# Set-up in finer steps over four engines, norms by ScalarE, last rows through TensorE, and a new order in every queue

## The reference

```python
x = x + attn(layernorm(x)); x = x + ffn(layernorm(x))
# attn, per sequence of 512 rows
q = tanh(xn @ W_charge.T + b)[..., 0];  phi_c = mags * q ** arange(5)
shell = xn @ W_shell.T + b_shell;  shell = shell / max(norm(shell), 1e-12)
proj = shell @ omega.T + rff_bias
phi_s = concat([cos(proj), sin(proj)]) * rff_scale
phi = (phi_c outer phi_s).reshape(.., 320) @ W_combine.T
logits = phi @ phi.T * decay / (softplus(log_temp) + 0.1), causal
out = softmax(logits) @ (xn @ W_v.T + b_v) @ W_out.T + b_out
# ffn: route each row to 64 slots (hidden gelu layer, top 8, softmax = alpha),
# gather rows into slots, one GRU step per slot, spread slot values by alpha
```

## Time and profile before

| | |
|---|---|
| median of 3 runs | 716.89 us (716.38 to 717.22) |
| the profiled execution, its own time | 718.19 us |
| its span, first to last instruction | 716.4 us |
| busy share of the span: PE, DVE, ACT, POOL | 96%, 85%, 70%, 57% |
| mean granted clock of PE | 0.994 |
| stages in the span | set-up and prologue to 190.9, twelve turns of the loop to about 682, end to 716.4 |

### The profile page before, as it was taken

One profiled execution on the slowest core, in us unless ns is written; L12 is line 12 of the kernel. 1 busy time (PEld: TensorE's weight loads), 2 busy tenths in 40 slices (PEclk: granted clock), 3 DMA queues, 4 the chain that ended last, 5 costly groups with the idle time before them and its releaser, 6 DMA issues.

```text
span 716.4 us, 15768 instructions
## 1 busy us (share of the span) xinstructions
PE 686.0 (96%) x4652; PEld 545.1 (76%) x4652; DVE 605.6 (85%) x1996; ACT 498.2 (70%) x1239; POOL 408.5 (57%) x861
## 2 busy tenths in 40 slices
PE   8988999999999999999999999999999999998895
PEld 4766787877796977888797878779687777876774
DVE  5868978788989898998989898898989899787965
ACT  3758896958486786858677695858679685856441
POOL 4646577454565667475665757476565747635300
PEclk8999999999999999999999999999999999999999
DMA  8241111202332140423224051323205032121004
GB/s 251 81 148 40 50 29 32 60 1 88 92 117 60 57 123 2 130 47 119 59 77 102 1 156 23 118 61 114 63 31 146 4 118 60 61 59 60 1 28 150
DMA packets 49114, 54.11 MB, mean 76 GB/s; under 512 B 6212, under 2 KB 40582, under 8 KB 49030
## 3 DMA queue, kind: packets, MB, share of 16 engines
q1 hardware_dynamic: 48258, 52.58, 25.9%
q10 hardware_dynamic: 772, 0.53, 0.3%
HBM read 20.58 MB, written 16.78 MB: 52 GB/s over the span
## 4 chain that ended last, share of the span: by engine, by line
PE 62%; ACT 16%; issue 8%; POOL 6%; DVE 3%; DMA 3%; SPq 1%; ACTq 1%; DVEq 0%; POOLq 0%
PE ps L340 16%; PE ps L314 12%; PE ps L432 6%; PE ps L509 5%; PE ps L406 4%; PE ps L573 4%; PE ps L494 4%; PE ps L385 4%; POOL Z L251 2%; ACT L724 2%; ACT Eh L755 2%; DMA xmT<-Z 2%; PE ps L460 2%; ACT L776 2%; PE ps L387 2%
## 5 line engine op out<-in xcount | busy, mean ns | idle before, releaser
L678 ACT ACTIVATE xn<-X,rs 128x255 f32<-128x255 f32 x128 | 66.2, 593 | 77.7 <-POOL rs L1299 77.7
L251 POOL TENSOR_TENSOR Z<-Z,QB 128x512 f32<-128x512 f32 x60 | 77.1, 1286 | 73.8 <-ACT Z L734 71.3
L432 PE MATMUL ps<-Vh,Eh 128*128 128x256 f32 x320 | 96.0, 300 | 2.6 <-DVE El L934 2.0
L340 PE MATMUL ps<-W1h,xh 128*128 128x354 f32 x256 | 88.3, 345 | 1.5 <-DVE Vl L890 1.4
L432 PE MATMUL ps<-Vh,El 128*128 128x256 f32 x320 | 89.4, 279 | 0.0
L432 PE MATMUL ps<-Vl,Eh 128*128 128x256 f32 x320 | 89.4, 279 | 0.0
L340 PE MATMUL ps<-W1h,xl 128*128 128x354 f32 x256 | 83.1, 325 | 0.0
L340 PE MATMUL ps<-W1l,xh 128*128 128x354 f32 x256 | 83.1, 325 | 0.0
L890 DVE TENSOR_TENSOR Vl<-ps,Vh 128x256 fp32r<-128x256 f32 x128 | 53.3, 419 | 35.0 <-ACT Vh L700 33.9
L745 ACT ACTIVATE E<-ps,nmax 128x128 f32<-128x128 f32 (+3 forms) x128 | 67.7, 531 | 15.7 <-DVE nmax L926 15.3
L934 DVE TENSOR_TENSOR El<-ps,Eh 128x128 fp32r<-128x128 f32 (+3 forms) x128 | 60.8, 484 | 7.4 <-ACT Eh L755 7.3
(11 more groups left out here) (213 smaller groups left out, 1990.5 us busy)
## 6 DMA issues: line engine op xcount, KB each, us to landing
X<-in_x SPq DMA_DIRECT2D x32, 512.0 KB, 4.5
xmT<-Z SPq DMA_DIRECT2D x120, 128.0 KB, 2.3
out_x<-X SPq DMA_DIRECT2D x30, 512.0 KB, 3.5
out_x<-X SPq DMA_DIRECT2D x4, 256.0 KB, 3.2
X<-in_gru_whhT SPq DMA_DIRECT2D x1, 768.0 KB
wih<-in_gru_wihT SPq DMA_DIRECT2D x1, 768.0 KB
X<-in_W_v ACTq DMA_DIRECT2D x1, 256.0 KB, 4.4
X<-in_W_outT ACTq DMA_DIRECT2D x1, 256.0 KB, 5.6
```

Source lines behind the costliest of these rows:

```text
L251: e.tensor_tensor(Z[:, i + 1, :], Z[:, i, :], QB[:, :], ALU.mult).then_inc(s["zm"], 1)
L340: ins = e.matmul(p[:, 0:FEATS], x[:, d, c, t * 128:t * 128 + 128], w[:, c, :], start=j == 0, stop=j == 5)
L432: ins = e.matmul(p[:, 0:D], w[:, r % 2, j * 128:j * 128 + 128], v[:, (2 * k + d) % 4, j, :], start=z == 0, stop=z == len(parts) - 1)
L678: ins = e.activation(xn[:, d, t, 0:D - 1], X[:, b % NX, t, 0:D - 1], ACT.Identity, bias=rs[:, d, 2, t:t + 1], scale=rs[:, d, 1, t:t + 1])
```

## The change

It touches five things; the sizes of all tiles stay.

1. Set-up. ACT's queue issues W_v, W_out, b_v, b_out, omega; the biases of shell and charge go to SP's queue, ahead of the second x. The signals are split: wv (W_v, b_v), wa (W_out, b_out, omega), wsh (shell). PE can start the value products when wv and wa are there. The copy to W1 is gone: high parts are cast from PSUM, one half by DVE, one by ACT (`weights_high`); low parts are taken from PSUM. POOL's nine constants go first. DVE's set-up is cut into `bias_setup`, `temper_setup`, `attention_setup`, `slot_setup`, three `slot_values_setup` and others, placed between steps of pairs 0 and 1. ACT empties the six state products (`states_setup`). PE gets `keep_warm` (256-column matmuls on zeros, one and four of them).
2. Norms. `square` and `norm_sum` are gone. `v_high` copies 34 columns and squares the 64 shell columns with a sum (`accum_out`).
3. `sine` takes the Sin of the remainder first, then Abs, then the second Sin.
4. End. `warm` 3, 4, 21 and 2 become one `warm(12)`. `residual` puts the last two row tiles of X in PSUM by an identity matmul, `out_mm` adds to them, and DVE and ACT copy one each (`last_copy`) in place of two `finish`.
5. Every queue has a new order in prologue, loop and end.

```diff
@@ v_high (ACT)
-                    e.wait_ge(s["sq"], b - 1)
+                    e.wait_ge(s["n2"], 8 * k)
+                    e.wait_ge(s["q1"], k)
-                e.activation(F[:, d, t, :], at["vs", b, t][:, D:FEATS], ACT.Copy)
+                e.activation(F[:, d, t, 64:98], at["vs", b, t][:, D + 64:FEATS], ACT.Copy)
+                e.activation(F[:, d, t, 0:64], at["vs", b, t][:, D:D + 64], ACT.Square,
+                             accum_out=n2[:, d, 0, t:t + 1]).then_inc(s["n2"], 1)
@@ the end (PE)
+                    ins = e.matmul(p[:, :], ident[:, :], X[:, (2 * k + d) % NX, 2:4, :].rearrange("p t d -> p (t d)"),
+                                   start=True, stop=False, skip_group_check=True)
+                ins.then_inc(s["res"], 1)
@@ start of PE's queue, after
+            first_warm(); weights_setup(); keep_warm(1); xn_t(0, 0, 0); xn_t(0, 0, 1); keep_warm(4)
+            proj(0, 0, 0); xn_t(0, 1, 0); xn_t(0, 1, 1); proj(0, 0, 1); proj(0, 0, 2); proj(0, 0, 3)
+            proj(0, 1, 0); proj(0, 1, 1); proj(0, 1, 2); xn_t(1, 0, 0); xn_t(1, 0, 1); proj(0, 1, 3)
+            slot_setup(); gates_setup(); states_setup(); xn_t(1, 1, 0); proj(1, 0, 0); q_t(0); proj(1, 0, 1)
+            xn_t(1, 1, 1); proj(1, 0, 2); proj(1, 0, 3); z_t(0); proj(1, 1, 0); phi(0); proj(1, 1, 1)
+            logits(0, 0); proj(1, 1, 2); e_t(0, 0); e_t(0, 1); proj(1, 1, 3); logits(0, 1); e_t(0, 2)
@@ start of DVE's queue, after
+            clear_setup(); values_setup(); ln_stats(0, 0, 0); ln_stats(0, 0, 1); scale_a_setup()
+            shell_setup(); ln_stats(0, 1, 0); ln_stats(0, 1, 1); ln_stats(1, 0, 0); scale_b_setup()
+            weights_high(); ln_stats(1, 0, 1); weights_low(0); weights_low(1); xn_low(0, 0, 0)
+            xn_low(0, 0, 1); v_low(0, 0, 0); xn_low(0, 1, 0); xn_low(0, 1, 1); v_low(0, 0, 1); v_low(0, 0, 2)
+            bias_setup(); v_low(0, 0, 3); ln_stats(1, 1, 0); temper_setup(); ln_stats(1, 1, 1); v_low(0, 1, 0)
+            v_low(0, 1, 1); slot_setup(); v_low(0, 1, 2); xn_low(1, 0, 0); slot_values_setup(0)
@@ start of POOL's queue, after
+            scales_setup(); ln_scale(0, 0); ln_scale(0, 1); attention_setup(); ln_scale(1, 0); temper_setup()
+            slot_setup(); ln_scale(1, 1); rnorm(0); phase(0); ln_scale(2, 0); rnorm(1); phase(1)
@@ loop, PE
-                xn_t(p, 0, 0); xn_t(p, 0, 1); gx_rz(m); e_t(n, 0); proj(p, 0, 0); proj(p, 0, 1); proj(p, 0, 2)
-                proj(p, 0, 3); xn_t(p, 1, 0); xn_t(p, 1, 1); gx_n(m); values(n, 0); xm_t(f, 0, 0)
+                xn_t(p, 0, 0); xn_t(p, 0, 1); gx_rz(m); e_t(n, 0); e_t(n, 1); proj(p, 0, 0); proj(p, 0, 1)
+                xn_t(p, 1, 0); proj(p, 0, 2); xn_t(p, 1, 1); proj(p, 0, 3); gx_n(m); values(n, 0)
@@ loop, ACT, the part behind the first tiles
-                v_high(p, 1, 2); expo(n, 4); v_high(p, 1, 3); xm_copy(f, 1, 0); expo(n, 5); charge(p)
-                xm_copy(f, 1, 1); gelu(f, 0); probs_t(n, 3); probs_t(n, 4); q_copy(p); gelu(f, 1); sine(p)
+                probs_t(n, 2); v_high(p, 1, 1); expo(n, 5); v_high(p, 1, 2); v_high(p, 1, 3); charge(p)
+                xm_copy(f, 1, 0); xm_copy(f, 1, 1); gelu(f, 0); probs_t(n, 3); probs_t(n, 4); q_copy(p)
+                gelu(f, 1); sine(p); rt_out(f); probs_t(n, 5); z_copy(p); expo(n, 6); expo(n, 7)
@@ loop, DVE, the first part
-                finish(g, 0, 0); row_max(n, 1); row_max(n, 2); xn_low(p, 0, 0); xn_low(p, 0, 1); row_max(n, 3)
+                row_max(n, 1); row_max(n, 2); row_max(n, 3); finish(g, 0, 0); xn_low(p, 0, 0); xn_low(p, 0, 1)
@@ end, PE
-            gx_rz(14); hidden(15, 1); al_t(14); route(15); gx_n(14); rt_t(15); out_mm(13, 1); warm(21)
+            xm_t(15, 0, 0); xm_t(15, 0, 1); gx_rz(14); xm_t(15, 1, 0); xm_t(15, 1, 1); hidden(15, 0)
+            hidden(15, 1); al_t(14); route(15); gx_n(14); rt_t(15); out_mm(13, 1); warm(12); residual()
```

More of the change, by code:

```diff
@@ L582, in first_warm, with keep_warm @@
                     e.matmul(banks[2][:, :], E[:, 0, 0:128], E[:, 0, :], start=True, stop=True)
+            def keep_warm(n):
+                for _ in range(n):
+                    e.matmul(banks[2][:, 0:256], E[:, 0, 0:128], E[:, 0, 0:256], start=True, stop=True)
             def warm(n):
@@ L594, in weights_setup @@
                     cs = slice(c * 128, c * 128 + 128)
[L595 to L597 removed]
+                    p = at["setup_mm", c]
                     columns_of(p, 256, [(wsc[:, cs], ident[0:65, 0:65])])
@@ L639, in _ @@
-            proj(4, 1, 1); proj(4, 1, 2); values(3, 0); proj(4, 1, 3); logits(3, 1); out_mm(0, 0); gather(1)
-            e_t(3, 2); hidden(2, 0); q_t(4); values(3, 1); values(3, 2); xm_t(2, 1, 0); e_t(3, 3)
-            xm_t(2, 1, 1); logits(3, 2); values(3, 3); hidden(2, 1); out_mm(0, 1); gi_t(1); e_t(3, 4)
-            e_t(3, 5); route(2); z_t(4); rt_t(2); gx_rz(1); values(3, 4); gx_n(1); e_t(3, 6); values(3, 5)
-            e_t(3, 7); al_t(1); values(3, 6); slot_v(1); values(3, 7); phi(4); gather(2); logits(4, 0)
@@ new lines, in _ @@
+            values(1, 7); phi(2); xn_t(4, 0, 0); proj(3, 0, 3); logits(2, 0); xm_t(1, 0, 0); proj(3, 1, 0)
+            e_t(2, 0); proj(3, 1, 1); proj(3, 1, 2); xm_t(1, 0, 1); proj(3, 1, 3); e_t(2, 1); e_t(2, 2)
+            values(2, 0); logits(2, 1); gather(0); values(2, 1); e_t(2, 3); q_t(3); hidden(1, 0)
+            xm_t(1, 1, 0); xm_t(1, 1, 1); values(2, 2); values(2, 3); gi_t(0); e_t(2, 4); hidden(1, 1)
+            xn_t(4, 0, 1); e_t(2, 5); gx_rz(0); values(2, 4); route(1); logits(2, 2); gx_n(0); z_t(3)
@@ new lines, in _ @@
+            e_t(2, 6); values(2, 5); al_t(0); xn_t(4, 1, 0); rt_t(1); values(2, 6); proj(4, 0, 0)
+            proj(4, 0, 1); proj(4, 0, 2); proj(4, 0, 3); e_t(2, 7); phi(3); xn_t(4, 1, 1); values(2, 7)
+            logits(3, 0); proj(4, 1, 0); proj(4, 1, 1); proj(4, 1, 2); e_t(3, 0); xm_t(2, 0, 0); proj(4, 1, 3)
+            e_t(3, 1); slot_v(0); values(3, 0); xm_t(2, 0, 1); e_t(3, 2); logits(3, 1); out_mm(0, 0)
+            gather(1); e_t(3, 3); values(3, 1); hidden(2, 0); q_t(4); xm_t(2, 1, 0); xm_t(2, 1, 1)
@@ new lines, in _ @@
+                xm_t(f, 0, 0); logits(n, 1); out_mm(g, 1); xm_t(f, 0, 1); proj(p, 1, 0); proj(p, 1, 1)
+                e_t(n, 2); proj(p, 1, 2); proj(p, 1, 3); values(n, 1); xm_t(f, 1, 0); xm_t(f, 1, 1)
+                hidden(f, 0); e_t(n, 3); values(n, 2); q_t(p); e_t(n, 4); hidden(f, 1); logits(n, 2); route(f)
+                e_t(n, 5); values(n, 3); z_t(p); rt_t(f); values(n, 4); values(n, 5); e_t(n, 6); e_t(n, 7)
+                slot_v(m); al_t(m); values(n, 6); values(n, 7); phi(p); gather(f); out_mm(m, 0); logits(p, 0)
```

525 lines of the change are left out of this document (273 added, 252 removed).

## The result

| | before | after |
|---|---|---|
| median | 717.06 us (716.38 to 717.32) | 728.42 us (726.65 to 728.77) |
| ratio | | 1.0127, interval 1.009 to 1.0163 |
| profiled execution, its span | 718.19 us, 716.4 | 728.77 us, 727.0 |
| start of phi(4), phi(5), phi(15) | 187.10, 227.86, 638.64 | 191.58, 233.06, 648.91 |
| from phi(15) to the end of the span | 77.76 | 78.09 |

The span grew by 10.6 us: 4.5 up to phi(4), 5.8 in the eleven turns from phi(4) to phi(15), 0.3 behind them. (The turns are the distances from one phi to the next in PE's timeline; single turns are longer by 0.2 to 1 us where phi waits for the moves of Z, in every kernel here, so medians are compared.)

The account below looks back on a forecast made before the run. PE was taken to bound the loop (40.59 of 41.0 us a turn), ACT a near second in one part. Prologue minus 3.0, loop plus 1.2, end minus 1.3 took 716.89 to 713.8 us; range 706.5 to 720.0.

Parts of the forecast that it names:

- Start and slot products: Set-up: first projection at 17.6 for 19.59 us (minus 2.0), slot products at 28.1 for 30.43 (minus 2.3).
- From the slot products to e_t(0, 0): Prologue, first attention: e_t(0, 0) near 51.5 for 57.41 us, a lead of 5.9 less 1.0, or 4.9.
- the bound of 0: Set-up, first projection: no gain if PE's clock falls in the new waits or the shell biases come late.
- Norms on ACT: All stages: ACT pays 0.24 us a tile (0.05 to 0.26), 1.9 us per turn, 31 us in all.
- Relief of POOL and DVE: Loop: the norm work taken off POOL and DVE, 613 and 409 ns per four tiles, gains 0.
- The loop: Twelve turns: plus 0.1 us per turn, plus 1.2 in all.
- rival C: Loop: ACT becomes the bound, from about 0.36 us extra wait per turn, turns above 41.4; 719.8 us, chance 0.20.
- Rest of the prologue: First attention to pair 5: ACT gives back 1.9 of the 4.9 us lead, 3.0 left at the loop.
- The end: End of the kernel: minus 1.3 us in sum, of it minus 0.8 at the last copies and stores; ends minus 2.5 and 0.
- E: Rival, ACT: Square brings table loads, two per tile, plus 328 us, 1042 us; chance 0.02.
- D: Rival, set-up: loads, POOL's chain or PE's clock eat the lead, prologue 0; 716.8 us, no change; chance 0.13.

Follow-up runs that it names:

- b_norms: The kernel before with only the norms moved to ACT (v_high squares with a sum, square and norm_sum gone), all orders old; ratio 1.0046, turns of 41.26 us.
- a_loop: The changed kernel with the old order in all five loops, norms still on ACT and the new sine kept; ratio 1.0063, turns of 41.40 us.
- the repeat: The changed kernel run again unaltered, against the kernel before in the same rounds; ratio 1.0099.
- a_both: The changed kernel with attended(n, 0) ahead of row_max(n, 4) and Abs ahead of the first Sin; ratio 1.0064, turns of 40.99 us.
- b_warm8: The kernel before with eight instead of six matmuls on zeros at PE's start; ratio 0.9986.
- b_warm9: b_warm8 plus eight matmuls of 128 columns on the identity in PE's wait ahead of the first e_t; ratio 0.9979 to the kernel before.
- b_warm9b: b_warm9 run again unaltered, a second time against the kernel before; ratio 0.9977.

## Why the prediction was wrong

*Start and slot products: right.* 17.05 us for the forecast 17.6, 27.40 for 28.1. But the reason given for the first was mostly wrong: with two more warm matmuls and no fall the old set-up has its first projection at 17.68, and b_norms, with the old set-up as it is and no fall there, at 17.85. I had noted that the 18 products of the fold ran mostly at the low clock, and put the whole 2.0 us down to the finer loads. A steady clock alone gives 1.7 to 1.9 of the 2.5 us measured; that the sum met the forecast was in part luck.

*From the slot products to e_t(0, 0): the first step that failed.* Forecast 51.5, measured 57.34. Of the 5.8 us, by the comparison with a_loop, 3.2 are the fall of the clock from 33.1 to 40.0 (state products plus 2.15, the projection and transposes behind them plus 1.06), 1.1 stood already ahead of the third slot product (with no fall till then; its cause is open), and 1.5 are left without a fall (52.99 for 51.5), among them that PE waits for DVE between the three banks, as I had seen, and 1.56 us for the first exponential. I had named a fall in the new waits as the bound of 0 for the first projection alone, and gave none for the waits between the slot products. And the lead was counted from 57.41, a time that holds 1.7 us of a fall of its own. The lead between two kernels with a steady clock is 2.7 us, not 5.9. And 57.34 is that one execution: the same kernel had its first e_t at 54.82 in the repeat, with a shorter fall.

*Norms on ACT: the price was too high, its place right.* 0.15 us a tile for the 0.24 I took (the range was 0.05 to 0.26), 1.2 us a turn for 1.9. The error was that the accumulator read counts 226 ns in its group, but the next instruction starts 0.09 us behind it:

```profile
L726 ACT ACTIVATION_READ_ACCUMULATOR F<-ps 128x1 f32 x128 | 28.9, 226 | 0.0
```

I had written that nothing shows this behind a PSUM source. The trace of the kernel before does show it, at the exponential:

```profile
427.22 0.19 ACT L745 ACTIVATION_READ_ACCUMULATOR E<-ps,nmax 128x1 f32 x1
427.31 0.68 ACT L745 ACTIVATE E<-ps,nmax 128x512 f32<-128x512 f32 x1
```

With the prices of the Trainium skill's ScalarE: Activation LUTs, section "What ACT_TABLE_LOAD costs", the prediction's estimate for a tile was 0.28 us; the section has none for the read, and 0.19 of that was the read. The trace has 0.15. Relief of POOL and DVE was worth 0 as said.

*The loop: plus 1.2 forecast, plus 6 measured; this is the larger error.* The terms that I had were not far off. The first projection of the turn came 0.2 us later, as forecast for `xn_low` behind four `row_max`; it was made up by the second `xm_t`, which starts 17.87 us behind phi in both kernels. sine cost 0.14 us for the 0.1. What was missing is a term, put at nothing without a reason: `attended(n, 0)` behind `row_max(n, 4)`, 0.33 us a turn. I followed the new order on ACT and the low parts on DVE, and not the bank that `proj(p, 1, 0)` takes, whose last reader is `attended(n, 0)`. The wait is a circle between two engines: DVE waits 0.81 us for PE's logits, and PE's next projection waits for what stands behind them on DVE. By size the turn landed in rival C's range (above 41.4), but C's mechanism, ACT as the bound, is not what happened: a_both has 41.0 with the same ACT work. That the norms alone cost 0.31 us a turn in the old order (b_norms) comes near C, but below its mark of 0.36, and the place isn't shown.

*Rest of the prologue: 1.9 given back forecast.* All of the lead and more is gone at phi(4), 4.5 us behind the kernel before. I had no term for the order there at all, nor for a lead that waits swallow. The norms (about 0.8) and the order (size unclear) may pay for it, but the old prologue kept only -0.3 to 1.1 of a lead of 1.7 to 1.8 (b_warm8, b_warm9, b_warm9b). How the 4.5 us split stays open. A part is that execution's: in the repeat, the same kernel had phi(4) at 188.46, not 191.58.

*The end: minus 1.3 forecast, plus 0.3 measured.* The last copy (DVE's, 0.68 us from 721.61) ends at 722.29 us, 38.10 us behind the start of gather(15), and was at 39.46 before (673.54 to 713.0): 1.36 earlier, as forecast. But the four stores are issued one after the other in 2.1 us from 721.1, and the first of them waits for the same `finish` as before. The fourth goes out at 723.2, 0.45 us earlier by the same measure, and the span ends 3.8 us behind it, for 3.4 before. I had written that their issue is late next, and still took 0.8. In front of gather(15) 0.34 us were lost in a longer wait for the slot values:

```profile
684.19 1.96 PE L486 MATMUL ps<-xm,AL 128*64 128x257 f32 x16 [1.52 <-DVE SV L1116]
```

```profile
673.54 1.96 PE L494 MATMUL ps<-xm,AL 128*64 128x257 f32 x16 [1.18 <-DVE SV L1065]
```

*E did not happen:* Square brought no table load (54 loads in both profiles). *D* had a part of the picture right (DVE and the clock eat into the lead) and the wrong sum: it gave the prologue 0, where 4.5 us were lost, and shared the loop's missing term.
